# Ramp loads on two queues in opposite quadrant orders, and one x rounded one step sooner

## What is computed

```python
x = x + einsum('bct,bcd->bdt', x, L0_cond_weights[itok_B_0_15])     # 32 x 128 x 2048
x = x + einsum('bsi,boi->bso', x, L1_cond_weight[itok_B_3_7])       # weight rows o, columns i
```

## Time and profile before

| | us |
|---|---|
| median of 3 runs (lowest, highest) | 1512.5 (1512.16, 1513.29) |
| the profiled execution's own time | 1514.39 |
| its span, first to last instruction | 1512.6 |
| TensorE busy | 1488.4 (98%) |
| GpSimd, VectorE, ScalarE busy | 1083.3, 1012.8, 514.0 |
| moved by DMA | 261.33 MB, 173 GB/s over the span |

### The profile page before, as it was taken

One profiled execution on the slowest core, in us unless ns is written; L12 is line 12 of the kernel. 1 busy time (PEld: TensorE's weight loads), 2 busy tenths in 40 slices (PEclk: granted clock), 3 DMA queues, 4 the chain that ended last, 5 costly groups with the idle time before them and its releaser, 6 DMA issues.

```text
span 1512.6 us, 28891 instructions
## 1 busy us (share of the span) xinstructions
PE 1488.4 (98%) x6534; PEld 1227.2 (81%) x6535; DVE 1012.8 (67%) x641; ACT 514.0 (34%) x786; POOL 1083.3 (72%) x659
## 2 busy tenths in 40 slices
PE   5999999999999999999999999999999999999998
PEld 4778888888888888888888888888888888888887
DVE  6682977959672589786676277977759419788521
ACT  2433333333333333333333333333333333333332
POOL 4766877768785788776777577777777667787653
PEclk9999999999999999999999999999999999999999
DMA  7796999979794698997978578989889758998543
GB/s 156 179 222 139 209 191 192 218 164 201 157 205 109 149 209 176 188 197 161 201 167 182 125 160 175 214 183 185 181 178 186 157 130 175 189 198 187 120 111 85
DMA packets 290918, 261.33 MB, mean 173 GB/s; under 512 B 19032, under 2 KB 211544, under 8 KB 290904
## 3 DMA queue, kind: packets, MB, share of 16 engines
q10 hardware_dynamic: 107712, 170.97, 49.1%
q1 hardware_dynamic: 183192, 90.22, 33.3%
HBM read 227.56 MB, written 33.55 MB: 173 GB/s over the span
## 4 chain that ended last, share of the span: by engine, by line
PE 93%; SPq 3%; issue 2%; POOL 2%; ACT 0%; DMA 0%; DVE 0%; ACTq 0%; POOLq 0%; DVEq 0%
PE z_ps L716 29%; PE z_ps L708 29%; PE z_ps L707 29%; SPq L204 2%; PE out_ps L728 2%; PE out_ps L725 2%; PE out_ps L726 2%; POOL x_low L264 1%; POOL z_low L270 0%; SPq L197 0%; POOL a_full L275 0%; DMA ids_row<-in_itok_B 0%; DMA x_nat<-in_x 0%; SPq L212 0%; ACT z_high L346 0%
## 5 line engine op out<-in xcount | busy, mean ns | idle before, releaser
L707 PE MATMUL z_ps<-w_high,x_high 128*128 x1984 | 773.0, 390 | 2.4 <-ACT x_high L339 1.8
L708 PE MATMUL z_ps<-w_low,x_high 128*128 x1984 | 772.8, 389 | 0.0
L264 POOL TENSOR_TENSOR x_low<-x_turn,x_high 128x1024 fp32r<-128x1024 f32 x248 | 624.4, 2538 | 36.0 <-ACT x_high L339 36.0
L582 DVE STREAM_TRANSPOSE x_turn<-x_nat 128x1024 f32<-128x1024 f32 x246 | 291.0, 1220 | 430.7 <-DMA x_nat<-in_x 430.5
L716 PE MATMUL z_ps<-w_high,x_low 128*128 x1984 | 469.9, 389 | 0.0
L707 PEld LDWEIGHTS z_ps<-w_high,x_high 128*128 128x128 f32 x1984 | 373.1, 188 | 80.6 <-issue 3.3
L708 PEld LDWEIGHTS z_ps<-w_low,x_high 128*128 128x128 f32 x1984 | 373.1, 188 | 77.3
L716 PEld LDWEIGHTS z_ps<-w_high,x_low 128*128 128x128 f32 x1984 | 372.5, 188 | 77.2
L270 POOL TENSOR_TENSOR z_low<-z_raw,z_high 128x512 fp32r<-128x512 f32 x127 | 168.2, 1324 | 212.2 <-ACT z_high L346 212.2
L354 ACT ACTIVATE out_sb<-out_ps 128x512 f32<-128x512 f32 x128 | 76.8, 600 | 598.1 <-PE out_ps L728 552.3
L339 ACT ACTIVATE x_high<-x_turn 128x1024 fp32r<-128x1024 f32 x248 | 251.9, 1061 | 53.3 <-DVE x_turn L582 47.5
(11 more groups left out here) (93 smaller groups left out, 301.4 us busy)
## 6 DMA issues: line engine op xcount, KB each, us to landing
x_nat<-in_x ACTq DMA_DIRECT2D x492, 256.0 KB, 5.2
w_nat<-in_L_cond_weight SPq DMA_DIRECT2D x320, 256.0 KB, 7.8
out<-out_sb ACTq DMA_DIRECT2D x128, 256.0 KB, 5.5
a_full<-in_L_cond_weights ACTq DMA_DIRECT2D x128, 64.0 KB, 5.2
x_nat<-in_x SPq DMA_DIRECT2D x96, 64.0 KB, 2.7
ids_row<-in_itok_B SPq DMA_DIRECT2D x1, 16.0 KB, 3.0
cond_i<-in_itok_B SPq DMA_DIRECT2D x1, 0.5 KB
expert_i<-in_itok_B SPq DMA_DIRECT2D x1, 0.5 KB
```

What stands on the lines that cost most here:

```text
L264: nc.gpsimd.tensor_tensor(x_low[s][:, half], x_turn[:, half], x_high[s][:, half], ALU.subtract)\
L582: nc.vector.transpose(x_turn[:].rearrange("p (k a c) -> p k a c", a=QUAD, c=SQ)[:, blocks], x_nat[:].rearrange("p (a k c) -> p k a c", a=Q ...
L707: nc.tensor.matmul(z_ps[s][:], xs, w_high[:, ds(at + k * NC, NC)], start=(k == 0), stop=False)
L708: nc.tensor.matmul(z_ps[s][:], xs, w_low[:, ds(at + k * NC, NC)], start=False, stop=False)
```

## The change

Three things change in the order in which work is asked for; what is computed stays. First, load_piece and load_x_quarter take the issuing engine and a tuple of quadrants. Piece 0 of w is asked for half by SyncE (quadrants 0, 1) and half by ScalarE (2, 3). After it SyncE has the later pieces and the quarters of x0 and x2, in the order 0, 1, 2, 3; ScalarE has those of x1 and x3, in the order 2, 3, 0, 1, each behind its own rounding of the quarter before, without a wait of its own. Each reads a sequence's number just before it needs it. The first two a loads move from before ScalarE's piece 0 to behind it. Second, GpSimd's second half of x4's low part moves behind z_low(1). Third, ScalarE's rounding of x5, with the load of x6, moves from behind z(3) to behind z(2), ahead of the load of a(4), out(2), a(3) and z(3).

```diff
--- before.py
+++ after.py
@@ -49,6 +49,7 @@
 HALF = KP * NC // 2
 RAMP = 4
 AHEAD = 2
+UP, DOWN = (0, 1), (2, 3)
 XQ = T // PIECES
 EXPERTS = 8
 MAXQ = 32
@@ -180,43 +181,49 @@
                               x[ds(b, 1), :, j * XF:(j + 1) * XF].rearrange("o (a p) f -> p (o a) f", p=SQ))\
                     .then_inc(x_loaded, DMA)
 
+        rows = w1.rearrange("e o i -> (e o) i")
+
+        def first_row(eng):
+            return eng.value_load(first_row_tab[:], min_val=0, max_val=rows.shape[0] - NC)
+
+        def first_seq(eng, s):
+            return eng.value_load(first_seq_tab[:, s:s + 1], min_val=0, max_val=B - 1)
+
+        def load_piece(eng, m, row, quads):
+
+            chunk = rows[ds(row, NC), :].rearrange("(a p) i -> p a i", p=SQ)
+            for j in quads:
+                i0 = j * XF + m * PF
+                eng.dma_start(w_nat[m % 2][j * SQ:(j + 1) * SQ, :].rearrange("p (a f) -> p a f", f=PF),
+                              chunk[:, :, i0:i0 + PF]).then_inc(w_loaded[m % 2], DMA)
+
+        def load_x_quarter(eng, m, s, b, quads):
+
+            for j in quads:
+                i0 = j * XF + m * PF
+                eng.dma_start(x_nat[j * SQ:(j + 1) * SQ, s * XQ:(s + 1) * XQ].rearrange("p (a f) -> p a f", a=QUAD),
+                              x[ds(b, 1), :, i0:i0 + PF].rearrange("o (a p) f -> p (o a) f", p=SQ))\
+                    .then_inc(xq_loaded[s], DMA)
+
         @block.sync
         def _(sp):
             sp.dma_start(ids_row[:], adapter.partition_broadcast(P)).then_inc(ids_loaded, DMA)
             sp.dma_start(cond_i[:], bass.AP(cond.tensor, 0, [[0, CHUNKS], [1, B], [1, 1]])).then_inc(own_loaded, DMA)
             sp.dma_start(expert_i[:], bass.AP(adapter.tensor, 0, [[0, CHUNKS], [1, B], [1, 1]])).then_inc(own_loaded, DMA)
-            rows = w1.rearrange("e o i -> (e o) i")
-
-            def load_piece(q, m, row):
-                chunk = rows[ds(row, NC), :].rearrange("(a p) i -> p a i", p=SQ)
-                s = m % 2
-
-                sp.wait_ge(w_turned, q * PIECES + m + 1)
-                for b in range(QUAD):
-                    i0 = b * (T // QUAD) + m * PF
-                    sp.dma_start(w_nat[s][b * SQ:(b + 1) * SQ, :].rearrange("p (a f) -> p a f", f=PF),
-                                 chunk[:, :, i0:i0 + PF]).then_inc(w_loaded[s], DMA)
-
-            def load_x_quarter(m, s, b):
-
-                for j in range(QUAD):
-                    i0 = j * XF + m * PF
-                    sp.dma_start(x_nat[j * SQ:(j + 1) * SQ, s * XQ:(s + 1) * XQ].rearrange("p (a f) -> p a f", a=QUAD),
-                                 x[ds(b, 1), :, i0:i0 + PF].rearrange("o (a p) f -> p (o a) f", p=SQ))\
-                        .then_inc(xq_loaded[s], DMA)
-
             sp.wait_ge(first_known, 1)
-            row0 = sp.value_load(first_row_tab[:], min_val=0, max_val=rows.shape[0] - NC)
-            load_piece(0, 0, row0)
+            row0 = first_row(sp)
+            load_piece(sp, 0, row0, UP)
             sp.wait_ge(first_known, 2)
-            seqs = [sp.value_load(first_seq_tab[:, s:s + 1], min_val=0, max_val=B - 1) for s in range(RAMP)]
-            for m in range(PIECES):
-                if m > 0:
-                    load_piece(0, m, row0)
-                for s in range(RAMP):
-                    if m > 0:
-                        sp.wait_ge(xq_turned, (m - 1) * RAMP + s + 1)
-                    load_x_quarter(m, s, seqs[s])
+            seqs = {}
+            for s in (0, 2):
+                seqs[s] = first_seq(sp, s)
+                load_x_quarter(sp, 0, s, seqs[s], UP + DOWN)
+            for m in range(1, PIECES):
+                sp.wait_ge(w_turned, m + 1)
+                load_piece(sp, m, row0, UP + DOWN)
+                for s in (0, 2):
+                    sp.wait_ge(xq_turned, (m - 1) * RAMP + s + 1)
+                    load_x_quarter(sp, m, s, seqs[s], UP + DOWN)
             sp.wait_ge(tables_made, 2)
             row1 = of_group(sp, ROW, 1, rows.shape[0] - NC)
             for i in range(AHEAD):
@@ -226,14 +233,17 @@
                         sp.wait_ge(xq_turned, (PIECES - 1) * RAMP + m + 1)
                     else:
                         sp.wait_ge(x_turned, 2 * (RAMP + i - 1) + m // 2 + 1)
-                    load_x_quarter(m, m, b)
-                load_piece(1, i, row1)
+                    load_x_quarter(sp, m, m, b, UP + DOWN)
+                sp.wait_ge(w_turned, PIECES + i + 1)
+                load_piece(sp, i, row1, UP + DOWN)
             for m in range(AHEAD, PIECES):
-                load_piece(1, m, row1)
+                sp.wait_ge(w_turned, PIECES + m + 1)
+                load_piece(sp, m, row1, UP + DOWN)
             with sp.Fori(2, count_groups(sp)) as q:
                 row = of_group(sp, ROW, q, rows.shape[0] - NC)
                 for m in range(PIECES):
-                    load_piece(q, m, row)
+                    sp.wait_ge(w_turned, q * PIECES + m + 1)
+                    load_piece(sp, m, row, UP + DOWN)
 
         @block.gpsimd
         def _(pool):
@@ -256,9 +266,9 @@
                                     pattern=[[-1, P]], channel_multiplier=1).then_inc(consts_made, 1)
             pool.wait_ge(consts_made, CONSTS)
 
-            def x_rest(t, s):
-
-                for h in range(2):
+            def x_rest(t, s, halves=(0, 1)):
+
+                for h in halves:
                     half = slice(h * T // 2, (h + 1) * T // 2)
                     pool.wait_ge(x_high_made, t * 2 + (h + 1))
                     nc.gpsimd.tensor_tensor(x_low[s][:, half], x_turn[:, half], x_high[s][:, half], ALU.subtract)\
@@ -292,9 +302,10 @@
                     a_rest(0, 0)
                     add_eye(1, 1)
             z_rest(0)
-            x_rest(4, 0)
+            x_rest(4, 0, (0,))
             a_rest(1, 1)
             z_rest(1)
+            x_rest(4, 0, (1,))
             add_eye(0, 2)
             a_rest(2, 0)
             z_rest(2)
@@ -378,9 +389,13 @@
 
 
 
-            act.wait_ge(tables_made, 2)
-            load_a(0, 0)
-            load_a(1, 1)
+            act.wait_ge(first_known, 1)
+            load_piece(act, 0, first_row(act), DOWN)
+            act.wait_ge(first_known, 2)
+            seqs = {}
+            for s in (1, 3):
+                seqs[s] = first_seq(act, s)
+                load_x_quarter(act, 0, s, seqs[s], DOWN + UP)
 
             def round_w(m, h):
 
@@ -404,6 +419,12 @@
                 round_w(m, 1)
                 for s in range(1, RAMP):
                     round_x_quarter(m, s)
+                    if s in seqs and m < PIECES - 1:
+                        load_x_quarter(act, m + 1, s, seqs[s], DOWN + UP)
+                if m == 0:
+                    act.wait_ge(tables_made, 2)
+                    load_a(0, 0)
+                    load_a(1, 1)
                 if m == 1:
                     take_a(0, 0)
                 if m == 2:
@@ -424,14 +445,14 @@
             take_a(2, 0)
             act.wait_ge(out_made, 2)
             take_z(2, 2)
+            take_x(5, 1)
+            load_x(6)
             act.wait_ge(a_split, 3)
             load_a(4, 0)
             take_out(2, 0, 1)
             take_a(3, 1)
             act.wait_ge(out_made, 3)
             take_z(3, 3)
-            take_x(5, 1)
-            load_x(6)
             act.wait_ge(a_split, 4)
             load_a(5, 1)
             take_out(3, 1, 1)
```

## The result

The changed kernel is slower, by about 3.9 us:

| | before | after |
|---|---|---|
| median of 18 runs each (lowest, highest), us | 1512.73 (1511.95, 1513.97) | 1516.64 (1514.26, 1519.61) |
| ratio of the times, 95% interval | | 1.0023 [1.0016, 1.0029] |
| the profiled execution's own time | 1514.39 | 1514.26 |
| its span | 1512.6 | 1512.4 |

The account below looks back on a forecast made before the run. TensorE, busy from 140 to 1500 us, bounds the kernel, so only the first 110 us can move. Ramp 3.0 + step 1 1.2 - step 2 2.05 - step 3 2.9 + x6 4.0 = 3.2 us saved: 1509.3, range 1505.5 to 1513.5.

Parts of the forecast that it names:

- the term of the ramp: Loads on two queues up to the end of step 0's product: 1.3 + 1.1 + 0.6 = 3.0 us gained.
- Step 2: VectorE's cast and difference hold off GpSimd: TensorE gaps of 1.8 and 0.85, 2.65 us for 0.6 before.
- the term of x6: x6 asked for at 73.0, not 78.53: step 6's gap, its half clock and a z_low wait go, +4.0 us.
- the clock: Half-clock spell taken to fall behind step 2's gap, where it is free; behind step 3's it would cost 1.6 us.
- The start: Piece 0 of w, split over two queues, lands sooner: first matmul gains 1.3 us, bounds 0 and 1.35.
- Pieces 1 to 3: Ramp: piece 1 there near 19.7; loss 0.5 for 1.6 before; in pieces 2 and 3 the 0.6 goes.
- A: Rival: the whole kernel comes out as forecast, 1509.3 us, from 1507.6 to 1510.4; chance 0.36.
- C: Rival: half clock behind step 3 (1510.9), w's first halves not overlapping (1510.6), or both (1512.2); chance 0.30.
- x4 and step 1: x4's second half no longer holds ScalarE's work for step 1's product with a: 1.2 us gained.
- x5 ahead: ScalarE waits at x5 before out(2) and z(3): step 3's product loses 2.9 us where there was none.
- D: Rival: ScalarE stands at x5, delaying out(2), z(3) and step 3's product: 1512.3 to 1517; chance 0.13.
- B: Rival: cast and difference fall between GpSimd's operations; steps 2 and 3 lose 1 to 3 us: 1504.5 to 1507; chance 0.21.

Follow-up runs that it names:

- Before again: The kernel before, unchanged, run once more for a second profile: 1513.22 us, span 1511.4.
- the queues alone: The changed kernel with GpSimd's half of x4's low part and ScalarE's x5 put back, leaving the two load queues: 1508.57 us, ratio 0.9972.
- after again: The changed kernel, unchanged, run once more for a second profile: 1516.11 us, span 1514.3.
- the kernel with both gaps filled: The changed kernel plus 25 matmuls with unused results in TensorE's waits at steps 2 and 3: 1515.02 us, ratio 1.0014.

## Why the prediction was wrong

It said 1509.3, from 1505.5 to 1513.5, 3.2 us faster; the kernel became 3.9 us slower. The step that failed first is the term of the ramp, 3.0 us forecast and 0.55 measured against the same profile (nothing against before's second one). Step 2's gap was stacked on it and came out larger. The second is the term of x6, +4.0, which was read from a gap and a spell that belonged in part to one execution. The third is the clock, put at nothing. The mechanisms at the steps 2 and 3 were right.

- **The start: 1.3 us forecast, 0.2 measured.** The chain "piece 0 landed, VectorE free, first matmul" is right, but w was used at 12.99, not 12.05. The rate taken between the rows, 300 GB/s, was too high: 263 from 8 to 12 us, and x0's loads share it now. VectorE had 0.42 us more to wait, for x0. The bounds given (0 to 1.35) hold it.
- **Step 0 on piece 0: not in the sum.** The forecast moved VectorE's work "as it is". x0 came 0.42 us late, GpSimd got the first turn, and the 12 matmuls took 1.26 us longer, most of it by the wider spacing of the last four, whose cause stays open. With this the 3.0 us of the ramp came out as 0.55 (61.68 to 61.13 for the product of step 0), and as 0 to 0.4 against before's second profile.
- **Pieces 1 to 3.** The prediction's list calls 21.44, 33.90 and 56.22 the starts of pieces; they are those of step 1 on the pieces 0, 1 and 3. Its counts of matmuls and its losses are right all the same. The losses forecast there were small (0.5 and 0), and they were. VectorE came to the pieces 1, 2 and 3 at 22.14, 33.26 and 43.10, 4 to 5 us sooner than before (26.19, 37.12, 48.48), but later than forecast (near 20 for piece 1): the forecast took the 6.9 us of a piece from the earlier trace rows as a fixed time, where the rows had the DMA engines slack, and with two queues they are saturated to 44 us. TensorE didn't wait for these pieces. The same saturation cost elsewhere: it made x0 late, and the first a load took 5.5 us from its issue (24.68) to its use (30.20), where 2.2 to 4.2 were estimated. The prediction had "bound by the transfer" as a rival "inside A and C", priced for piece 1 alone.
- **x4 and step 1: 1.2 us forecast, right.** The product of step 1 has no gap.
- **Step 2: 2.65 us of gaps forecast, 3.3 measured.** The cause and the instructions named are those of the trace. As the ramp had gained less, z_low(1) began at 64.56, not 62.1, and so the cast had its turn ahead of x_low's second half, not behind it. The half then stood between the cast and the difference, and a_full ended at 71.66 and a_low began at 72.08, where the forecast had a_full done by 67.3 and a_low begun at 69.5.
- **x5 ahead: the product of step 3 2.9 us late, right as a mechanism.** ScalarE's 3.5 us from the first issue to the copy was 3.52 (74.45 to 77.97), z_high ended 2.46 behind the copy. z_low was later than counted, held behind w_low (a_low took 1.72 us for 0.46). Alone, this move costs 5.6 us, not 2.9.
- **x6: +4.0 forecast. Step 6 waits no more, but 1.9 of it wasn't there to win.** The sum was made against the profiled execution (1514.4, so 1511.2 for after), and then the whole saving was taken off the median of 1512.5. The 1.9 us by which the profiled execution lay above the median were its own, and the second profile shows where 1.2 of them lay. Before again lost 2.9 us between the starts of step 5 and of its product's third matmul where the first profile lost 4.1, and had no spell. And in the queues alone x6's gap is gone too, without x5's move.
- **The clock: one spell, free, forecast.** In the profile shown it was so: a spell where TensorE would have waited. In after again there are two, and the second is not hidden. Over the runs, by the kernel with both gaps filled, it costs 1.6 us.
- The sum, again: forecast against its own profile 1511.2, measured in its kind 1514.3 to 1516.1. Ramp 2.45 short, step 2 0.65 short: 3.1 us, which is the 3.15 by which step 5 began late (84.60 for 81.45). The clock's 1.6 and the 1.9 of the wrong base are what separates 1509.3 from 1516.6 beyond that, with some 0.7 left unexplained.

Of the rivals, D had the right side with a chance of 0.13, and its place: ScalarE at x5. It asked for x5 turned past 75.5 before the kernel would be slower; x5 was turned at 73.75. The point from which it decides lay sooner, because all that it stacked on had gained less. The measured 1516.64 is in D's upper end, beyond 1515.5, which had 0.05. Both conditions of C came about as well: the first matmul stayed near 16.65 (16.45), and after again has the spell behind step 3. B's did not: the two engines met.

Two rules of the Trainium skill bear on the ramp. Page "SBUF — State Buffer", section "Can I just issue two DMAs to hit both halves?", has two transfers on the two halves of the partitions at 6% more than one. Measured here: 263 GB/s against 235 in 8 to 12 us, 12%, with x0's first loads in the same stretch. Here the measurement decides, but in time the page was nearer than the forecast's 300 GB/s: 0.3 us by the page (an estimate), 0.2 measured, 1.3 forecast. The quadrant order adds nothing to it (258 and 267 with one order). Page "DMA: Bandwidth & Descriptors", section "Issuing engines are not separate DMA queues", says that a second issuing engine saves the issuing time and nothing else. The traces agree as far as they go: from 20 to 44 us the second engine took the rate from 194 to 216 GB/s, up to a share of 1.23, and the queues alone gain 4.3 us, with everything behind the ramp asked for some 4 us sooner (w's next piece at 56.03 for 60.43). No run parts the time saved on the queue from the new order of the loads.

## What to carry to other kernels

Before an operation of GpSimd is moved, write down what VectorE runs beside it: where the two take turns, a step of 0.46 us costs 2.5, and the order of VectorE's work is worth as much thought as GpSimd's (here x5 turned first, 5.4 us, in part because x5 was then ready sooner). Work that waits for a transfer must not be put ahead of copies that TensorE waits for; first ask whether an earlier load brings it in time where it is. And hold a sum against a second profile of the kernel before, as a gap and its half-clock spell can be of that one execution: here the two profiles differ by 0.55 us at the end of the ramp and by 1.2 at step 6, as much as what was to be gained.

## What was not expected of the chip

- With the DMA engines saturated, four loads per quarter in opposite quadrant orders moved 236 to 249 GB/s from 12 to 16 us (12 traces), in one order 218 and 220; from 20 to 44 us 213 to 218 against 225 and 219. On the queues alone this was worth no time.
- A gap of 2.2 us on TensorE was followed by half clock in the profile of the kernel with GpSimd's half moved, and the mean clock was below 0.999 in 4 of its 11 runs, not in the other 7. With unused matmuls in the gap it was so in none of 11.
- TensorE's first matmuls stand 0.39 to 0.47 us apart, twice the usual 0.23, up to 20.5 us before and 22.5 us after, while the clock's row reads 1.00. In a spell whose row reads 0.50 they stand 0.43 apart.
- The turns of VectorE and GpSimd chain: the difference took 4.37 us for 2.29, and the operation of 0.46 behind it 2.50. The page "SBUF — State Buffer" of the Trainium skill, section "SBUF: two separate sides", has the lock held for a whole instruction, and the trace agrees. In these rows the turn went each time to the one that stood.
